# One graph-network block on one core: edge transfers in halves, finer waits in the reduction trees, one more chunk's sums on TensorE, first group merged tile by tile

## The chip, the cores and the metric

One core of a Trainium2 chip. The metric is the device time of one execution in microseconds, the median of several.

## The reference

Inputs are 6250 nodes with 256 features, 200,000 edges with 96 features, sorted by destination, and the weights of three layers. What is computed:

```
xn   = layernorm(x)                                   # (6250, 256)
sum, max, cnt = segment sum / max / count of edge_attr_96 by dst      # (6250, 96) each
h    = [xn, sum, max (0 where cnt = 0), sum / max(cnt,1), u]          # 256+3*96+64
gnn  = relu(h @ W1 + b1) @ W2 + b2 + xn
q,k,v = split(xn @ Wqkv + bqkv);  q, k centred by row, squared, normalised
mix  = (v + q2 @ (k2^T @ v) / sqrt(N)) @ Wout + bout                  # linear attention
x1   = x + gnn + mix
xm   = layernorm(x1);  w = xm @ wr + br
the 3124 nodes of largest w get  gelu(xm @ w1 + b1) @ w2 + b2, times w, on top
out  = x1 + xm + (that, for chosen nodes)
```

All of it in float32, or in products of split float32 parts (high and low) on TensorE.

## The kernel before, in words

**Edges.** The edges are padded to 448 x 448 = 200,704 = 128 x 1568 rows. Each partition holds 1568 consecutive edges, cut into 49 chunks of 32 edges. Four edges make a quad. `edge_chunk(c)` on VectorE works on one chunk of 128 x 32 x 96 in a buffer `xb` (four of them): a tree of two steps for the maximum (L995 into `mx`, L999) and two for the sum (L998, L1002, in place) reduces each quad to one row, and then a running segmented scan goes over the chunk's eight quads: for each quad a maximum (L1018) and a sum (L1021), each with a per-partition flag that restarts a segment, into `ob` (two buffers). The semaphore `s_tree` counts tree steps, `s_max` and `s_sum` count scan steps. Before its tree a chunk waits for its load (`s_load`), and before its scan for the dump of the chunk two back (`s_dump`), and for all four tree steps.

SyncE loads chunk c + 4 and dumps chunk c to `scan_d` in DRAM once chunk c is scanned (`dump_and_load`): one dump of 768 KB and one load of 1536 KB a chunk, in this order in its queue. Between chunks 36 and 41 SyncE adds loads of W1 (four pieces), W2 (two) and the tail rows.

**Sums on TensorE.** For the chunks in `SUMS` (1, 2, and 44 to 48) VectorE leaves the two sum steps out. `quad_sums(c)` on TensorE adds the four edges of each quad with identity matmuls, four quads (a half) into one PSUM bank. The sum scan then reads PSUM. Chunks 1 and 2 share the banks `psKx`, the late ones `psR` and `psC`, so each half waits until the chunk before has been scanned that far.

**Nodes, beside the edges.** ScalarE takes the root for the layer norm (L1555), behind two small DMA issues (L1551, L1553) that wait for VectorE. VectorE finishes the deviations, and goes on with chunk 1. TensorE and ScalarE then go over 12 groups of 4 tiles of 128 nodes and one tile more: transposes, queries and keys, the base rows, key products. VectorE gives key norms at fixed chunks (`NORM`), the last two behind chunks 32 and 33. GpSimd gathers neighbour rows of destinations, from which ScalarE and VectorE find each node's segment.

After chunk 35 VectorE gives the factors `s_fac`, and TensorE and ScalarE do the attention product of the 13 groups: fetch 512 KB of `qT_d` on ScalarE's queue (four buffers), product, scaled copy, store 512 KB to `att_d` on the same queue. Between groups `WORK` spreads the rounding of the weights to a high part (ScalarE, `h0` to `h5`) and low parts (TensorE product and ScalarE copy, `l0` to `l11`). `h4` and `h5` need both W2 loads. `quad_sums(44)` stands behind group 10. The sums of chunks 45 to 48 stand behind the last attention group, its evacuation and a product with `endrow`, with one piece of the W1 tail product (`tail_part(0)` to `(3)`) behind each; ScalarE copies these out (`tail_rows`).

**Ramp into the node stage.** GpSimd gathers the raw first and last quads of group 0's segments (`raw0`). ScalarE waits for the last attention store, copies tail parts 0 and 1, rounds the node columns, then masks raw rows: 24 products into `graw[1]` (L1773) and 24 into `kept` (L1779). Behind these it issues the loads of `xTr[1]`, `bg` and `tg` (L1783, L1786), and copies tail parts 2 and 3. VectorE, once chunk 48 is scanned, makes a scan over partitions for segments that cross them (L1085 to L1088, L1262), then `aggregate(0, 0, 0, 2)`, `carries()`, `aggregate` parts 3 and 4 over all four tiles at once, `repair()` of rows in `scan_d`, and `aggregates_low`. GpSimd gathers the scan rows of group 0 (`grow`) with one semaphore for the four when all dumps have landed, then the row for the repair, the raw rows of group 1, writes the repair, four small constants, and goes on with the gathers of later groups. TensorE does the node products of group 0 for four pieces, transposes all four tiles of merged rows, and goes on with `turn(0, 4)`.

**Node stage and last network.** Thirteen turns on TensorE: hidden layer in split products, output in split products; VectorE, ScalarE and GpSimd merge the next group's edge rows beside it. Then the selection of nodes, and the last network over the chosen ones.

## Time and profile before

| | |
|---|---|
| median of 3 runs | 1180.55 us (1180.41 to 1182.44) |
| the profiled execution | 1180.66 us |
| its span, first to last instruction | 1178.9 us |
| busy: TensorE, VectorE, ScalarE, GpSimd | 1051.5, 991.9, 500.4, 451.9 us |
| mean granted TensorE clock | 0.938 |
| moved by DMA | 234.99 MB, mean 199 GB/s |

The times of all rows are microseconds from the start of the span. The span is 1.8 us shorter than the execution. Busy shares are averages over stages: VectorE's comes from the edge chunks (to 492 us), TensorE's from the node stage behind them.

### The profile page before, as it was taken

How to read it: one execution, taken by the hardware profiler on the slowest of the kernel's cores; microseconds unless marked ns; L12 is line 12 of the kernel's file. 1: busy time of each engine (PE TensorE's matmuls, PEld its weight loads, DVE VectorE, ACT ScalarE, POOL GpSimd, SP SyncE). 2: the span in 40 equal slices, each digit the busy share in tenths (PEclk: the TensorE clock that was granted, in tenths of full speed). 3: DMA queues.
4: the chain of work that ended last, by engine and by line, in shares of the span. 5: the costliest groups of instructions: out<-in, count | busy, mean ns of one | idle time of the engine just before them, and what ended most of it. 6: DMA issues, size and time to landing. Idle time of an engine off the chain costs nothing.

```text
span 1178.9 us, 16127 instructions
## 1 busy us (share of the span) xinstructions
PE 1051.5 (89%) x4683; PEld 781.9 (66%) x4683; DVE 991.9 (84%) x2410; ACT 500.4 (42%) x1487; POOL 451.9 (38%) x344
## 2 busy tenths in 40 slices
PE   2598999999988759888999999999999986799996
PEld 1355555656635536466888888888888972488886
DVE  7899999999999997966988889888897757576574
ACT  3547877778832422611332233322333323243341
POOL 0088810888300002076565445654443000223331
PEclk9798999999996979979999999999999996599998
DMA  9799999999988999533443333433333130111110
GB/s 344 288 318 371 346 376 365 356 376 360 335 315 330 415 418 366 189 120 90 133 148 127 123 102 126 150 124 125 107 102 123 54 108 17 38 37 42 46 43 20
DMA packets 76512, 234.99 MB, mean 199 GB/s; under 512 B 13105, under 2 KB 43094, under 8 KB 70178
## 3 DMA queue, kind: packets, MB, share of 16 engines
q1 hardware_dynamic: 42786, 157.00, 35.7%
q0 software_dynamic: 14224, 33.61, 10.0%
q10 hardware_dynamic: 19440, 43.66, 9.9%
q8 instruction: 26, 0.43, 0.2%
q14 instruction: 36, 0.29, 0.1%
HBM read 153.68 MB, written 80.55 MB: 199 GB/s over the span
## 4 chain that ended last, share of the span: by engine, by line
PE 49%; DVE 3%; POOL 2%; issue 1%; DMA 0%; ACT 0%; DVEq 0%; POOLq 0%
PE psR L70 5%; PE psC L70 5%; PE psQ L59 5%; PE psQ L60 5%; PE psKx L59 5%; PE psQ L61 5%; PE psKx L60 5%; PE psKx L61 5%; PE psR L71 3%; PE psC L71 2%; PE psT L2168 1%; PE psQ L2189 1%; PE psKx L2189 1%; POOL graw L474 1%; PE psR L69 1%
## 5 line engine op out<-in xcount | busy, mean ns | idle before, releaser
L474 POOL DMA_INDIRECT graw<-in_edge_attr,ic x90 | 128.7, 1430 | 33.1 <-issue 24.1
L1018 DVE SCALAR_TENSOR_TENSOR ob<-ob,mQ,mx 128x96 f32<-128x96 f32 x392 | 122.3, 312 | 13.4 <-PE psR L1943 6.5
L684 POOL DMA_INDIRECT near<-in_dst,rowi x49 | 87.8, 1792 | 63.8 <-DVEq L924 49.1
L1818 ACT ACTIVATE hT_hi<-psQ 128x512 fp32r<-128x512 f32 (+2 forms) x52 | 29.9, 575 | 186.0 <-PE psQ L2189 142.5
L684 POOL DMA_INDIRECT near<-ends_d,blki x49 | 82.3, 1679 | 68.0 <-DVEq L915 53.4
L1021 DVE SCALAR_TENSOR_TENSOR ob<-ob,kQ,xb 128x96 f32<-128x96 f32 x336 | 104.5, 311 | 0.0
L1970 PE MATMUL psQ<-Wqk,xT 128*128 128x512 f32 (+1 forms) x196 | 94.3, 604 | 0.0
L995 DVE TENSOR_TENSOR mx<-xb 128x1536 f32<-128x1536 f32 x49 | 85.6, 1747 | 1.2 <-DVE carry L1076 0.2
L998 DVE TENSOR_TENSOR xb<-xb 128x1536 f32<-128x1536 f32 x42 | 73.8, 1758 | 1.4
L500 POOL DMA_INDIRECT grow<-scan_d,ic x49 | 54.0, 1101 | 42.8 <-DMA scan_d<-ob 28.1
L70 PE MATMUL psR<-W2w,hT_hi 128*128 128x512 f32 x175 | 65.7, 411 | 3.9 <-DVE x L1184 3.9
L1818 ACT ACTIVATE hT_hi<-psKx 128x512 fp32r<-128x512 f32 (+2 forms) x52 | 29.8, 575 | 88.8 <-PE psKx L2189 88.7
L788 POOL DMA_INDIRECT out_x<-zo,lst x25 | 24.6, 986 | 104.7 <-DVE zo L1474 104.7
L70 PE MATMUL psC<-W2w,hT_hi 128*128 128x512 f32 x168 | 60.8, 399 | 0.0
L1991 PE MATMUL psKx<-xn,kc 128*128 128x257 f32 (+1 forms) x196 | 52.3, 390 | 5.2 <-ACT kc L1594 5.2
L480 POOL DMA_INDIRECT yg<-yrow_d,lst x25 | 24.9, 997 | 82.0 <-DVE lst L1426 74.7
L746 POOL COPY ic<-idx 128x12 int32 (+3 forms) x11 | 4.5, 407 | 134.5 <-PE psC L69 134.5
L1970 PEld LDWEIGHTS psQ<-Wqk,xT 128*128 128x128 f32 (+1 forms) x196 | 38.0, 194 | 26.9 <-issue 24.3
L1982 PE MATMUL psC<-WvoI,xT 128*128 128x256 f32 (+1 forms) x196 | 50.6, 381 | 0.0
L71 PE MATMUL psR<-W2w,hT_lo 128*128 128x256 f32 x175 | 49.9, 285 | 0.0
L71 PE MATMUL psC<-W2w,hT_lo 128*128 128x256 f32 x168 | 47.4, 282 | 0.0
L1174 DVE SCALAR_TENSOR_TENSOR hT_lo<-psQ,hT_hi 128x512 fp32r<-128x512 f32 (+2 forms) x52 | 34.0, 654 | 15.3 <-ACT hT_hi L1818 15.3
(533 smaller groups left out, 3284.4 us busy)
## 6 DMA issues: line engine op xcount, KB each, us to landing
xb<-in_edge_attr SPq DMA_DIRECT2D x49, 1536.0 KB
scan_d<-ob SPq DMA_DIRECT2D x49, 768.0 KB
yrow_d<-yr SPq DMA_DIRECT2D x48, 132.0 KB
xg<-in_x ACTq DMA_DIRECT2D x12, 512.0 KB
xT_d<-xT ACTq DMA_DIRECT2D x12, 512.0 KB
base_d<-dcur ACTq DMA_DIRECT2D x12, 512.0 KB
qT_d<-qT ACTq DMA_DIRECT2D x12, 512.0 KB
out_x<-xres SPq DMA_DIRECT2D x48, 128.0 KB
```

The costliest lines, as they stand in the source:

```text
L59: nc.tensor.matmul(out, lh, rh, start=start, stop=False)
L60: nc.tensor.matmul(out, lh, rl, start=False, stop=False)
L61: return nc.tensor.matmul(out, ll, rh, start=False, stop=stop)
L70: nc.tensor.matmul(out, lh, both.rearrange("p h n -> p (h n)"), start=start, stop=False)
L71: return nc.tensor.matmul(out[:, 0:NF], ll, both[:, 0, :], start=False, stop=False)
L474: nc.gpsimd.indirect_dma_start(out=to.rearrange("p i f -> p (i f)"), out_offset=None, in_=raw_v, in_offset=bass.IndirectOffsetOnAxis(ap=ic ...
L684: nc.gpsimd.indirect_dma_start(out=near[:, t, :], out_offset=None, in_=table, in_offset=bass.IndirectOffsetOnAxis(ap=rows[:, t:t + 1], axi ...
L995: nc.vector.tensor_tensor(mx[:, :, :, :], xp[:, :, :, 0, :], xp[:, :, :, 1, :], ALU.max).then_inc(s_tree, 1)
L998: nc.vector.tensor_tensor(xp[:, :, :, 0, :], xp[:, :, :, 0, :], xp[:, :, :, 1, :], ALU.add).then_inc(s_tree, 1)
L1018: nc.vector.scalar_tensor_tensor(o[:, q, 0:EF], prev[:, 0:EF], mQ[:, bass.ds(c * TQ + q, 1)], mx[:, q, 0, :], ALU.min, ALU.max).then_inc(s ...
L1021: nc.vector.scalar_tensor_tensor(o[:, q, EF:AGG], prev[:, EF:AGG], kQ[:, bass.ds(c * TQ + q, 1)], quad_sum, ALU.mult, ALU.add).then_inc(s_ ...
L1970: ins = nc.tensor.matmul(o, xT[:, c, t * P:t * P + rows], Wqk[:, c, :], start=False, stop=(c == KF - 1))
```

## The change

- **Transfers in halves.** Loads and dumps of a chunk become two each, of 16 edges or 4 quads a partition. For each half of the scan done, SyncE issues half a dump and half a load. All semaphore counts double.
- **Trees.** The first sum step no longer waits for the first maximum step; each later step waits for the one two back; the scan's first maximum waits for the maximum tree, its first sum for the sum tree.
- **Roots sooner.** ScalarE's root stands ahead of the two small DMA issues.
- **Chunk 2's sums.** First half into `psR`, issued behind chunk 1's sums without a wait for its scan; second half into `psKx[0]`, issued inside TensorE's first node turn.
- **Chunk 42's sums** go to TensorE, behind attention group 9; those of 44 behind group 10, of 45 ahead of the last group. Tail part 0 now stands behind 46, part 1 behind 47, parts 2 and 3 behind 48.
- **Weights.** W1 in two pairs behind chunks 36 and 37, W2 behind 38 and 39, tail rows behind 40. `h4` and `h5` two groups later, `l8` to `l11` one later. The rows to gather are found behind chunk 38 instead of 39.
- **Ramp.** GpSimd makes the constants before the scan gathers; each tile's scan gather has its own semaphore. VectorE merges what doesn't need scan rows first, then tile by tile (`first_rows`): the zero for a node without edges comes through `unkept`, the mean from the mean of the other parts. TensorE transposes two tiles, does the fourth piece of node products, then the other two tiles. The loads of `xTr[1]`, `bg`, `tg` move from ScalarE's queue to SyncE's.

The core of the diff:

```diff
-SUMS_LATE = (44, 45, 46, 47, 48)
+SUMS_LATE = (42, 44, 45, 46, 47, 48)
...
-            psS = {c: psKx if c in SUMS_EARLY else [psR, psC] for c in SUMS}
+            psS = {c: [psR, psC] for c in SUMS_LATE}
+            psS[SUMS_EARLY[0]], psS[SUMS_EARLY[1]] = psKx, [psR, psKx[0]]
...
-            WORK = {4: ("h0",), 5: ("h1", "l0", "l1"), 6: ("h2", "l2", "l3"), 7: ("h3", "l4", "l5"), 8: ("h4", "l6", "l7"),
-                    9: ("h5", "l8", "l9"), 10: ("l10", "l11")}
+            WORK = {4: ("h0",), 5: ("h1", "l0", "l1"), 6: ("h2", "l2", "l3"), 7: ("h3", "l4", "l5"), 8: ("l6", "l7"),
+                    10: ("h4", "l8", "l9"), 11: ("h5", "l10", "l11")}
...
                 def dump_and_load(c, b, load):
-                    sp.wait_ge(s_sum, c * TQ + TQ + 1)
-                    sp.wait_ge(s_max, c * TQ + TQ + 1)
-                    sp.dma_start(scan_v[:, quads(c), :], ob[b % OB][:, :, :]).then_inc(s_dump[b % OB], 16)
-                    if load:
-                        sp.dma_start(xb[b][:, :, :, :].rearrange("p q i f -> p (q i) f"),
-                                     ev[:, bass.ds(c * T + XB * T, T), :]).then_inc(s_load[b], 16)
+                    for h in range(2):
+                        sp.wait_ge(s_sum, c * TQ + 4 * h + 5)
+                        sp.wait_ge(s_max, c * TQ + 4 * h + 5)
+                        sp.dma_start(scan_v[:, bass.ds(c * TQ + 4 * h, 4), :], ob[b % OB][:, 4 * h:4 * h + 4, :]).then_inc(s_dump[b % OB], 16)
+                        if load:
+                            sp.dma_start(xb[b][:, 4 * h:4 * h + 4, :, :].rearrange("p q i f -> p (q i) f"),
+                                         ev[:, bass.ds(c * T + XB * T + 16 * h, 16), :]).then_inc(s_load[b], 16)
...
-                pool.wait_ge(s_dump[0], 16 * 25)
-                pool.wait_ge(s_dump[1], 16 * 24)
-                gather_scan(0, GT, P, s_g0s)
+                pool.wait_ge(s_dump[0], 16 * 50)
+                pool.wait_ge(s_dump[1], 16 * 48)
+                for t in range(GT):
+                    nc.gpsimd.indirect_dma_start(
+                        out=grow[0][:, t, :], out_offset=None, in_=scan_d,
+                        in_offset=bass.IndirectOffsetOnAxis(ap=ic[0][:, 2, t:t + 1], axis=0)).then_inc(s_g0[t], 16)
...
                     nc.vector.tensor_tensor(mx[:, :, :, :], xp[:, :, :, 0, :], xp[:, :, :, 1, :], ALU.max).then_inc(s_tree, 1)
+                    if not on_pe:
+                        dve.wait_ge(s_tree, n0)
+                        nc.vector.tensor_tensor(xp[:, :, :, 0, :], xp[:, :, :, 0, :], xp[:, :, :, 1, :], ALU.add).then_inc(s_tree, 1)
                     dve.wait_ge(s_tree, n0 + 1)
-                    if not on_pe:
-                        nc.vector.tensor_tensor(xp[:, :, :, 0, :], xp[:, :, :, 0, :], xp[:, :, :, 1, :], ALU.add).then_inc(s_tree, 1)
                     nc.vector.tensor_tensor(mx[:, :, 0, :], mx[:, :, 0, :], mx[:, :, 1, :], ALU.max).then_inc(s_tree, 1)
...
-                    dve.wait_ge(s_tree, n0 + (2 if on_pe else 4))
+                    dve.wait_ge(s_tree, n0 + (2 if on_pe else 3))
...
+                        if q == 0 and not on_pe:
+                            dve.wait_ge(s_tree, n0 + 4)
...
+                    def first_rows():
+                        each = rcnt[:, 0:GT].rearrange("p (t o) -> p t o", o=1).broadcast_to([P, GT, EF])
+                        step(nc.vector.tensor_tensor(graw[0][:, :, 1, :], graw[0][:, :, 1, :], graw[0][:, :, 2, :], ALU.add), False)
+                        step(nc.vector.tensor_tensor(kept[:, :, 0, :], kept[:, :, 0, :], kept[:, :, 1, :], ALU.max))
+                        step(nc.vector.tensor_tensor(graw[0][:, :, 2, :], graw[0][:, :, 1, :], each, ALU.mult))
+                        for t in range(GT):
+                            dve.wait_ge(s_g0[t], 48)
+                            sums, mean_ = grow[0][:, t, EF:AGG], graw[0][:, t, 2, :]
+                            nc.vector.tensor_tensor(agg[:, t, EF:2 * EF], kept[:, t, 0, :], grow[0][:, t, 0:EF], ALU.max).then_inc(s_lead, 1)
+                            nc.vector.tensor_tensor(agg[:, t, 0:EF], graw[0][:, t, 1, :], sums, ALU.add).then_inc(s_lead, 1)
+                            nc.vector.scalar_tensor_tensor(agg[:, t, 2 * EF:3 * EF], sums, rcnt[:, t:t + 1], mean_, ALU.mult, ALU.add).then_inc(s_lead, 1)
...
                     aggregate(0, 0, 0, 2)
+                    dve.wait_ge(s_am, 2)
+                    dve.wait_ge(s_as, 2)
+                    step(nc.vector.tensor_tensor(kept[:, :, 1, :], kept[:, :, 1, :], kept[:, :, 2, :], ALU.max), False)
+                    step(nc.vector.tensor_tensor(graw[0][:, :, 2, :], graw[0][:, :, 2, :], graw[0][:, :, 3, :], ALU.add))
                     carries()
-                    for part in range(3, 5):
-                        aggregate(0, 0, 0, part)
+                    first_rows()
+                    for t in range(2):
+                        aggregates_low(0, t)
                     repair()
+                    for t in range(2, GT):
+                        aggregates_low(0, t)
...
+                act.wait_ge(s_ln, 1)
+                nc.scalar.sqrt(sd[:, :], va[:, :]).then_inc(s_sqrt, 1)
                 act.wait_ge(s_bw, 2)
...
+                QUADS_BEHIND = {9: 42, 10: 44}
...
+                quad_sums(45)
                 attention(GROUPS, 0, GROUPS // 4 * 16 + 16)
...
-                for i in range(4):
-                    quad_sums(SUMS_LATE[1 + i])
+                for i in range(3):
+                    quad_sums(46 + i)
                     tail_part(i)
+                tail_part(3)
...
-                    for m in range(4):
+                    for m in range(3):
                         hidden_nodes(0, m)
-                    transposes(0, range(GT))
+                    transposes(0, range(2))
+                    hidden_nodes(0, 3)
+                    transposes(0, range(2, GT))
```

## Rows read from the trace of the kernel before

**Rows 1.** Two stretches: us, TensorE, weight loads, VectorE, ScalarE, GpSimd busy (x), PEclk, DMA share, GB/s

```profile
200.00:250.00 50.00, 50.00 (x205) 31.50 (x204) 49.05 (x117) 36.85 (x130) 39.85 (x23) 1.00 0.97 360
420.00:440.00 20.00, 6.82 (x27) 4.58 (x25) 19.22 (x60) 3.91 (x8) 0.00 (x0) 0.80 1.03 415
```

**Rows 2.** Who waited for whom: us in total, times, longest

```profile
DVE ob L1018 <- PE psR L1943: 6.5, 1, 6.5
DVE a L901 <- ACT sd L1555: 2.2, 1, 2.2
DVE ob L1018 <- PE psC L1943: 1.4, 4, 0.5
DVE ob L1018 <- PE psKx L1943: 1.3, 2, 0.8
...
ACT W2w L1717 <- DMA rW<-in_L_gnn_W: 15.0, 1, 15.0
```

**Rows 3.** VectorE's timeline, chunk 34: start, us, line, operation, idle before

```profile
349.36 1.74 DVE L995 TENSOR_TENSOR mx<-xb 128x1536 f32<-128x1536 f32 x1
351.14 1.76 DVE L998 TENSOR_TENSOR xb<-xb 128x1536 f32<-128x1536 f32 x1
352.81 0.95 DVE L999 TENSOR_TENSOR mx<-mx 128x768 f32<-128x768 f32 x1
353.68 0.95 DVE L1002 TENSOR_TENSOR xb<-xb 128x768 f32<-128x768 f32 x1
354.72 0.32 DVE L1018 SCALAR_TENSOR_TENSOR ob<-ob,mQ,mx 128x96 f32<-128x96 f32 x1
...
358.40 1.75 DVE L995 TENSOR_TENSOR mx<-xb 128x1536 f32<-128x1536 f32 x1
```

**Rows 4.** VectorE's timeline: end of chunk 35, chunks 47 and 48, merging

```profile
367.45 0.16 DVE L1055 TENSOR_SCALAR kcol<-kcol 128x2 f32<-128x2 f32 x1
...
479.07 1.76 DVE L995 TENSOR_TENSOR mx<-xb 128x1536 f32<-128x1536 f32 x1
...
485.55 1.75 DVE L995 TENSOR_TENSOR mx<-xb 128x1536 f32<-128x1536 f32 x1
...
496.12 1.36 DVE L1120 TENSOR_TENSOR kept<-kept 128x1152 f32<-128x1152 f32 x1 [0.35 <-DVE carry L1262]
...
505.77 0.56 DVE L1128 TENSOR_TENSOR kept<-kept,grow 128x384 f32<-128x384 f32 x1 [4.78 <-issue]
```

**Rows 5.** ScalarE's timeline: the root's table load, the masking

```profile
45.75 1.28 ACT L1555 ACT_TABLE_LOAD   x1 [2.03 <-DVEq L867]
...
479.61 6.48 ACT L1773 ACTIVATE graw<-raw,kSel 128x96 f32<-128x96 f32 x24
485.99 8.69 ACT L1779 ACTIVATE kept<-raw,unkept,kSel 128x96 f32<-128x96 f32 x24
```

**Rows 6.** TensorE's timeline: first node group, tail product, group 0's edge products, turn 0

```profile
62.37 0.60 PE L1956 MATMUL psT<-ident,xn 128*128 128x128 f32 x4
...
476.26 1.02 PE L2103 MATMUL psQ<-rW1t,ident 96*98 96x512 f32 x2
...
477.99 2.42 PE L1943 MATMUL psR<-xb,ident 128*128 128x384 f32 x7
...
515.33 0.77 PE L59 MATMUL psQ<-aggT_hi,W1f_hi 128*128 128x512 f32 x1 [1.49 <-DVE tailT L1160]
...
548.36 0.80 PE L70 MATMUL psR<-W2w,hT_hi 128*128 128x512 f32 x1 [3.92 <-DVE x L1184]
```

**Rows 7.** SyncE's timeline: the first W load and the fifth

```profile
379.97 1.99 SPq L596 DMA_DIRECT2D rW<-in_L_gnn_W  x2
...
407.65 0.44 SPq L599 DMA_DIRECT2D rW<-in_L_gnn_W  x1
```

**Rows 8.** DMA issues in 376 to 380 and 405 to 412: KB each, us to landing

```profile
rW<-in_L_gnn_W SPq DMA_DIRECT2D x1, 512.0 KB, 11.7
rW<-in_L_gnn_W SPq DMA_DIRECT2D x1, 512.0 KB, 22.7
```

More of the change, by code:

```diff
@@ L488, in wait_chosen @@
                 if g == 0:
-                    engine.wait_ge(s_g0[t], 32 + 16)
+                    engine.wait_ge(s_g0[t], 48 + 16)
                 elif t == 0:
@@ L604, in _ @@
                         sp.dma_start(ub[GF:GF + 1, :], b1.rearrange("(a b) -> a b", a=1)).then_inc(s_wl[5], 16)
+                sp.wait_ge(s_at, 6 + KF + 12 * GT)
+                for e in range(4):
+                    sp.wait_ge(s_t2o[e], 16 * (GROUPS // 4 + (e == 0)))
+                for t in range(GT):
+                    sp.wait_ge(s_g0[t], 48)
+                sp.dma_start(xTr[1][:, :, :], xT_d[1:2, :, :, :].rearrange("o p c n -> p (o c) n")).then_inc(s_ld[1], 16)
+                for e in range(2):
+                    for to, src in ((bg[e], base_d), (tg[e], att_d)):
+                        sp.dma_start(to[:, :, :].rearrange("p t f -> p (t f)"), src[e * P:(e + 1) * P, :]).then_inc(s_lb[e], 16)
                 def node_stage():
@@ L1067, in _ @@
                         ends_of_segments()
-                    if c == 39:
+                    if c == 38:
                         rows_to_gather()
@@ L1076, in _ @@
                         step(nc.vector.memset(carry[:, 2 * EF:2 * EF + 1], 1.0))
+                        step(nc.vector.tensor_tensor(unkept[:, :, 5], unkept[:, :, 5], has[:, 0:GT], ALU.mult))
                         dve.sem_inc(s_lead, 1)
@@ L1274, in node_stage @@
                     dve.wait_ge(s_u, 1)
-                    for t in range(GT):
-                        aggregates_low(0, t)
                     selection_constants()
@@ L1933, in _, with quad_half @@
                 ins.then_inc(s_wv, 1)
+                def quad_half(c, h):
+                    pe.wait_ge(s_load[c % XB], c // XB * 32 + 32)
+                    group = SUMS_EARLY if c in SUMS_EARLY else SUMS_LATE
+                    k = group.index(c)
+                    if c == SUMS_EARLY[1]:
+                        pe.wait_ge(s_bw, 2)
+                        if h == 1:
+                            pe.wait_ge(s_sum, SUMS_EARLY[0] * TQ + 5)
+                    elif k:
+                        pe.wait_ge(s_sum, group[k - 1] * TQ + 4 * h + 5)
+                    for i in range(4):
+                        ins = nc.tensor.matmul(psS[c][h][:, 0:4 * EF], ident[:, :], xb[c % XB][:, 4 * h:4 * h + 4, i, :],
+                                               start=(i == 0), stop=(i == 3))
+                    ins.then_inc(s_wv if c in SUMS_EARLY else s_pt, 1)
                 def quad_sums(c):
-                    pe.wait_ge(s_load[c % XB], c // XB * 16 + 16)
                     for h in range(2):
-                        if c not in (SUMS_EARLY[0], SUMS_LATE[0]):
-                            pe.wait_ge(s_sum, (c - 1) * TQ + 4 * h + 5)
-                        for i in range(4):
-                            ins = nc.tensor.matmul(psS[c][h][:, 0:4 * EF], ident[:, :], xb[c % XB][:, 4 * h:4 * h + 4, i, :],
-                                                   start=(i == 0), stop=(i == 3))
-                        ins.then_inc(s_wv if c in SUMS_EARLY else s_pt, 1)
+                        quad_half(c, h)
                 def transpose_nodes(g, t):
@@ L2017, in turn @@
                         base(g, t)
+                        if g == 0 and t == 0:
+                            quad_half(SUMS_EARLY[1], 1)
                         if t + 2 < nt:
@@ L2029, in _ @@
                 pe.wait_ge(s_wrb, 3)
-                for c in SUMS_EARLY:
-                    quad_sums(c)
+                quad_sums(SUMS_EARLY[0])
+                quad_half(SUMS_EARLY[1], 0)
                 pe.wait_ge(s_wq, 1)
@@ L2136, in _ @@
                 nc.tensor.matmul(psT[0][:, :], ones[:, :], endrow[:, :], start=True, stop=True).then_inc(s_t, 1)
-                for i in range(4):
-                    quad_sums(SUMS_LATE[1 + i])
+                for i in range(3):
+                    quad_sums(46 + i)
                     tail_part(i)
+                tail_part(3)
                 pe.wait_ge(s_max, CHUNKS * TQ + 1)
@@ L2159, in transposes @@
                         for t in tiles:
-                            if t == 0:
+                            if isinstance(g, int) and g == 0:
+                                pe.wait_ge(s_lead, 2 + 5 * (t + 1))
+                            elif t == 0:
                                 pe.wait_ge(s_am, g * NAM + NAM)
```

72 lines of the change are left out of this document (38 added, 34 removed).

## The prediction

> **What bounds the kernel now.** I read the page's slices first, then the busy time by stretches, the waits, and last the timelines of the engines around the places that the change touches. From 50 to 492 us VectorE is the bound: in a typical stretch it is busy 49.05 of 50 us, and it folds one edge chunk after another [rows 1]. Afterwards TensorE is (100 us busy in 100 from 600 to 900). So the time is the end of the edge chunks, plus a ramp in which TensorE waits for the first group's merged rows, plus two stages that the change leaves alone. The ramp's end, H, is TensorE's first edge product of group 0, at 515.33 [rows 6]. What the change is worth is how far H moves, plus what it does to one stall behind H.
>
> VectorE's own waits inside the edge stage are few: 2.2 us for ScalarE's root, 1.3 for the sums of chunk 2, 6.5 and 1.4 for late chunks' sums [rows 2]. It never waits for a load or a dump, though the DMA engines are busy 0.97 to 1.03 of the time and move 360 to 415 GB/s [rows 1]. That is cover which can be used up, and the change uses some of it.
>
> **Start.** ScalarE's table load for the root begins at 45.75, behind two DMA issues that wait for VectorE, and VectorE waits 2.2 us for it [rows 2, 5]. The root now goes ahead of both, so about 2.0 of that go. Chunk 2's first half of sums gets a bank of its own and no longer waits for chunk 1, and TensorE reaches its second half at about 54 instead of VectorE needing it at 59: the 1.3 us go. TensorE's first node group starts near 50 instead of 62.37 [rows 6]; with the half inserted in it its lead is about 8.6 us. That gains nothing by itself. It lets TensorE keep up with a VectorE that is 12 us earlier where the key norms (chunks 32, 33) release it.
>
> **Trees.** In a chunk folded by VectorE the four tree instructions start at 349.36, 351.14, 352.81, 353.68 and the scan at 354.72 [rows 3]. The steps behind a wait for the instruction just ahead are 1.78 and 1.04; those without such a wait are 1.67 and 0.87. Reordered, each wait has another instruction in between: 1.78 becomes 1.67 and 1.04 becomes 0.87, 0.28 us a chunk. Bounds: 0, if the sum scan then exposes the same latency (it comes 1.10 behind the last sum, and 1.04 was enough), and 0.28. I take 0.28, on the 41 chunks that stay on VectorE: 11.5 us.
>
> **Chunk 42 on TensorE.** 9.04 us a chunk [rows 3] becomes 6.48, as chunk 47 takes from 479.07 to 485.55 [rows 4]: 2.6 us. TensorE pays about 5.3 (a half is eight passes, seven take 2.42 [rows 6]), in a stretch where it idles.
>
> **Late sums.** The 6.5 us wait came from chunk 45's sums queued behind the last attention group and its evacuation, and that behind a 15.0 us wait of ScalarE for the W2 rows [rows 2]. Now W2 is requested a chunk earlier and rounded two groups later, and 45's sums go ahead of that group. 6.5 us go. The 1.4 of small waits for psC I leave in: TensorE's 5.3 plus 1.7 of tail product (476.26 to 477.99 [rows 6]) still make some 7 us a chunk against 6.48. Moving the gather rows from chunk 39 to 38 changes no sum; one small multiply adds 0.1.
>
> So without DMA effects the last chunk would end 2.0 + 1.3 + 11.5 + 2.6 + 6.5 - 0.1 = 23.8 us earlier.
>
> **What the DMA gives back.** SyncE's queue lags in the attention stage. The first W row, issued at 379.97, lands 11.7 later; the one at 407.65 takes 22.7 [rows 7, 8]. Between these landings (391.7 and 430.4) that queue moved 0.52 MB of W1 and three times 2.88 MB (dump, load, W), 9.2 MB in 38.7 us: 237 GB/s. A chunk of 9.04 us asks for 318. Before, the prefetch of three chunks covered it. Now chunks ask every 8.76 us, and the full wait for the dump two chunks back bites first, since its second half stands behind half a load. My ledger: chunk 35 ends at 367.45 [rows 4] less 12.8 = 354.6; the factors and small work keep their lengths; chunk 40 ends at 404.2 and chunk 41's scan wants dump 39 at 409.3. The queue delivers the second W1 pair at 394.2, W2's first half at 406.4, and dump 39 (1.57 MB on) at 413.0: 3.7 us late. Dump 40 is 0.4 late, later ones are not, as ScalarE's queue then runs dry. The raw rows' gathers now fall into the same stretch; I give them 1. Sum 5.0, bounds 0 (the queue gets more than 237) and 10 (it gets 200). Chunk 48 ends 18.8 us earlier, about 473.5. Issuing in halves by itself costs SyncE some 1.7 us in 8.8 and waits for nobody.
>
> **The ramp.** Here I expect a loss that pays for the merging. ScalarE's masking (6.48 and 8.69 us) starts at 479.61 before, just behind the second tail product [rows 5, 6]. That product now stands behind chunk 47's sums instead of 46's, and those can't finish before chunk 46 is scanned: half a sum 1.8 us before its end, then 5.3, 0.4 of lag, 1.7 of product, 1.6 of ScalarE's copies, so masking starts 7.2 us after chunk 46, not 1.3 (that chunk ended 0.8 ahead of 479.07 [rows 4]). It ends 8.5 us behind the last chunk (492.3: chunk 48 from 485.55, 6.48 and small waits [rows 4]) instead of 2.4, and VectorE's merging, which began 3.8 behind it at 496.12, starts 4.8 later [rows 4]. From there H came 19.2 us later, 4.8 of which VectorE waited for the scan rows (at 505.77 [rows 4]). That wait is gone: half dumps and gathers behind single tiles have landed long before. The pieces added (two steps ahead of the carries, three in front of the tiles, twenty small ones) take 5.7 us against 4.2 of whole-group ones, but the first two tiles' transposes and casts run beside the last ones. I cost that as even: H is 14.4 behind the start of merging. H moves by 18.8 - 4.8 + 4.8 = 18.8 us. Bounds of the ramp's own part: 4.8 better (ScalarE in time), 3 worse. ScalarE loses 2.2 us of DMA issues; that helps TensorE's node products start, not H. SyncE's loads of group 0 and 1 now come after masking and gathers, wanted 30 us later.
>
> **Behind H.** TensorE waits at 548.36, 3.92 us for VectorE and that for GpSimd's addition, which is the end of an unbroken row of gathers [rows 6]. GpSimd now starts its scan gathers sooner and is 1.3 us earlier against H. Its iotas moved into an idle stretch. So 1.3 us go: 1180.66 (the profiled execution, 0.1 over the median of the runs) less 18.8 + 1.3 = 20.1 gives 1160.5. The node stage and the last network I leave as they are.
>
> **A page's rule.** While SyncE's queue moves its 237, all queues move about 415 [rows 1]: some 178 go to the others, ScalarE's rows of 4 KB a partition above all, against SyncE's of 12 and 6 KB. The Trainium skill (DMA: Bandwidth & Descriptors, Queues, rings and completion order) says that each DMA engine takes turns between queues packet by packet. By that rule halved edge packets cost SyncE's queue part of its share; the second rival below is this mechanism.
>
> **Rivals.**
> *No DMA lateness, or ScalarE not late in the ramp.* For it: no wait for a dump or load stands in the profile. Against: the 22.7 us landing. It gives back 5 to 6: 1155. Chance 0.17.
> *Halved packets lose turns.* Loads and dumps are then nearer in size to the other queue's rows, and the 237 fall to some 205. Dump 39 is 8 us late instead of 3.7: 1165. For it: a third to a half of the rate goes to a queue that has far smaller rows. Against: no row shows who is served in which order, and 237 may be what SyncE's transfers get whatever their size. Chance 0.15.
> *The edge stage is already DMA-bound.* The share of 0.97 to 1.03 then means no spare rate, and faster trees only wait. 34 chunks times 0.28 = 9.5 are lost: 1170. Against it: 415 GB/s in one stretch, 360 in the other [rows 1]. Chance 0.10.
> *Slower: halves lower the DMA rate.* A chunk needs 2.36 MB, and the node groups some 0.8 MB, in 8.76 us: 361 GB/s from chunk 3 on. Above that nothing is lost; at 338 the 299 us of chunks 3 to 35 grow by 20 and the gain is gone; at 330 the time is 1189. That is a fifth under the 415 shown. Chance 0.05, with small other mishaps. The same skill page (Rules for kernel authors) advises 1 MiB or more per DMA for full bandwidth, which speaks against halves; no row here shows a cost of 768 KB transfers.
> *Nothing measurable,* because gains are given back in an unread place: 1180, 0.03.
> My forecast: 0.50, own range 1156 to 1165.
>
> **How the numbers follow.** 1160.5 is the likeliest. With the first rival 1153 is the low end, with the packet and bound cases 1170 the high one; under 0.2 lie outside. A difference under 0.2% (2.4 us) can't be told from none. Faster 0.92, same 0.03, slower 0.05.
>
> **What would show it.** Tree steps of 1.67 and 0.87 throughout; the root's wait and chunk 2's gone; chunk 35 ending near 354.6. Waits of VectorE for a dump around chunk 41, 3 to 5 us. Masking starting some 7 us behind chunk 46, and VectorE's first merge waiting for ScalarE. H near 496.5; the stall of 3.92 us near 2.6. I am wrong if chunks of 8.76 us don't appear from chunk 3 on, if the last chunk ends after 480, or if the stretch behind H takes other than 662 to 664 us.

## Result: 4% slower, and the profile after

| | before | after |
|---|---|---|
| time, median | 1181.21 us (4 runs) | 1228.35 us (1224.36 to 1231.53, 4 runs) |
| profiled execution, span | 1180.66, 1178.9 us | 1231.53, 1229.6 us |
| H, TensorE's first edge product of group 0 | 515.33 [rows 6] | 567.80 |

The ratio is 1.0396, 95% interval 1.0358 to 1.0435: slower, where I had forecast 1160.5 us, faster. All of it lies ahead of H. The stretch behind H fell from 663.6 to 661.8 us. One stray execution each of two kernels below, 3618.39 and 2101.27 us, counts in the median of its kernel and not in its ratio; without it these medians are 1176.59 instead of 1177.58 and 1171.51 instead of 1172.41 us.

The waits of the changed kernel (engine and line waiting <- what ended the wait: us in total, times, longest) show where VectorE stands now. Of these lines, the first three had no counterpart before; the wait for psR was 6.5 us and the one for ScalarE's root (tile sd) 2.2 us [rows 2].

```profile
DVE rk L1048 <- ACT junk L1655: 61.1, 5, 29.2
...
DVE ob L1036 <- DMA scan_d<-ob: 10.3, 2, 5.6
...
DVE kept L1141 <- ACT kept L1824: 4.6, 1, 4.6
...
DVE ob L1036 <- PE psR L1989: 2.2, 2, 1.4
DVE cT L1106 <- PE psC L2199: 2.2, 1, 2.2
...
DVE a L918 <- ACT sd L1597: 0.3, 1, 0.3
```

VectorE waits 61.1 us for ScalarE's sums of squares, which make the keys' norms: no such wait stood in the profile before. ScalarE's own waits lead one step further back, to GpSimd's gathers:

```profile
ACT jc L1561 <- DMA near<-ends_d,blki: 33.1, 4, 17.2
ACT jc L1570 <- DMA near<-in_dst,rowi: 28.4, 2, 21.7
```

The gathered rows (tile near) show why they are late. First the kernel before: count, duration of an issue min/median/max in ns, first and last start.

```profile
L684 POOL DMA_INDIRECT near<-ends_d,blki x49: 943/1484/3890, 57.4 to 153.3; - x49
L684 POOL DMA_INDIRECT near<-in_dst,rowi x49: 1015/1486/3891, 203.4 to 302.0; - x49
```

The same two groups in the changed kernel:

```profile
L694 POOL DMA_INDIRECT near<-ends_d,blki x49: 940/1365/8447, 56.3 to 194.4; - x49
...
L694 POOL DMA_INDIRECT near<-in_dst,rowi x49: 940/1361/8442, 228.9 to 352.4; - x49
```

Same count, a lower median, but a longest issue of 8.4 us instead of 3.9: 138.1 and 123.5 us from first to last start instead of 95.9 and 98.6. VectorE and GpSimd side by side, in the changed kernel:

```profile
102.02 1.44 POOL L694 DMA_INDIRECT near<-ends_d,blki  x1 [0.30 <-issue]
103.76 8.44 POOL L694 DMA_INDIRECT near<-ends_d,blki  x1 [0.30 <-issue]
112.50 8.43 POOL L694 DMA_INDIRECT near<-ends_d,blki  x1 [0.30 <-issue]
```
```profile
106.22 1.75 DVE L1012 TENSOR_TENSOR mx<-xb 128x1536 f32<-128x1536 f32 x1
107.89 1.75 DVE L1015 TENSOR_TENSOR xb<-xb 128x1536 f32<-128x1536 f32 x1
109.56 0.95 DVE L1017 TENSOR_TENSOR mx<-mx 128x768 f32<-128x768 f32 x1
110.43 0.95 DVE L1020 TENSOR_TENSOR xb<-xb 128x768 f32<-128x768 f32 x1
111.30 0.31 DVE L1036 SCALAR_TENSOR_TENSOR ob<-ob,mQ,mx 128x96 f32<-128x96 f32 x1
```

The trees do what I predicted: steps of 1.67, 1.67, 0.87 and 0.87, 8.74 us from tree to tree (106.22 to 114.96). But an issue that begins 2.46 us ahead of a tree (103.76) now ends at 112.20, in the scan behind it; the next begins at 112.50, at the same place in the pattern, and is as long. Before, the longest one began 1.33 us ahead of a tree and ended 0.78 us into the second step:

```profile
90.48 3.89 POOL L684 DMA_INDIRECT near<-ends_d,blki  x1 [0.30 <-issue]
```
```profile
91.81 1.75 DVE L995 TENSOR_TENSOR mx<-xb 128x1536 f32<-128x1536 f32 x1
93.59 1.76 DVE L998 TENSOR_TENSOR xb<-xb 128x1536 f32<-128x1536 f32 x1
95.27 0.95 DVE L999 TENSOR_TENSOR mx<-mx 128x768 f32<-128x768 f32 x1
```

Between 91.81 and 93.59 lie 1.78 us instead of 1.67: the gap of 0.11 that the change took away. And where VectorE sits idle for the norms, each issue takes 0.94 us (the nine that begin from 124.91 to 134.89 all do). A stretch of the changed kernel with such a wait, columns as in [rows 1]: VectorE is busy 8.02 of 20 us.

```profile
120.00:140.00 20.00, 2.94 (x14) 1.71 (x13) 8.02 (x22) 6.18 (x24) 16.34 (x13) 0.65 0.68 208
```

The ramp, in VectorE's, ScalarE's and TensorE's timelines, as in [rows 4 to 6]:

```profile
552.55 1.36 DVE L1141 TENSOR_TENSOR kept<-kept 128x1152 f32<-128x1152 f32 x1 [4.62 <-ACT kept L1824]
```
```profile
537.25 6.47 ACT L1818 ACTIVATE graw<-raw,kSel 128x96 f32<-128x96 f32 x24
543.63 8.68 ACT L1824 ACTIVATE kept<-raw,unkept,kSel 128x96 f32<-128x96 f32 x24
```
```profile
567.80 0.47 PE L59 MATMUL psQ<-aggT_hi,W1f_hi 128*128 128x512 f32 x1 [1.49 <-DVE tailT L1181]
...
599.14 0.79 PE L70 MATMUL psR<-W2w,hT_hi 128*128 128x512 f32 x1 [5.17 <-DVE x L1205]
```

### The profile page after: what moved, and what is told of

It reads as the page before. It is cut to its first block, busy times and chain, and to the rows that moved or that the text cites. A ratio compares the mean times of both kernels' runs of the same rounds, so it can differ in the third digit from the quotient of the medians.

```text
span 1229.6 us, 16562 instructions
## 1 busy us (share of the span) xinstructions
PE 1062.3 (86%) x4699; PEld 787.4 (64%) x4699; DVE 984.4 (80%) x2424; ACT 502.0 (41%) x1487; POOL 533.9 (43%) x344
## 4 chain that ended last, share of the span: by engine, by line
PE 47%; DVE 3%; POOL 1%; issue 1%; DMA 0%; ACT 0%; DVEq 0%; POOLq 0%
PE psR L70 5%; PE psC L70 5%; PE psQ L59 4%; PE psQ L60 4%; PE psQ L61 4%; PE psKx L59 4%; PE psKx L60 4%; PE psKx L61 4%; PE psR L71 3%; PE psC L71 2%; PE psT L2225 1%; PE psQ L2246 1%; PE psKx L2246 1%; POOL graw L472 1%; PE psR L69 1%
## 5 line engine op out<-in xcount | busy, mean ns | idle before, releaser
L694 POOL DMA_INDIRECT near<-ends_d,blki x49 | 124.4, 2539 | 66.9 <-DVEq L932 52.3
L694 POOL DMA_INDIRECT near<-in_dst,rowi x49 | 117.3, 2394 | 48.1 <-DVEq L941 33.5
L1036 DVE SCALAR_TENSOR_TENSOR ob<-ob,mQ,mx 128x96 f32<-128x96 f32 x392 | 122.3, 312 | 14.1 <-DMA scan_d<-ob 10.3
L2020 PE MATMUL psQ<-Wqk,xT 128*128 128x512 f32 (+1 forms) x196 | 95.9, 613 | 0.0
L70 PE MATMUL psR<-W2w,hT_hi 128*128 128x512 f32 x175 | 66.2, 414 | 5.2 <-DVE x L1205 5.2
L2056 PE MATMUL psT<-ident,q 128*128 128x128 f32 (+1 forms) x98 | 19.0, 307 | 49.9 <-ACT qT L1696 49.7
L70 PE MATMUL psC<-W2w,hT_hi 128*128 128x512 f32 x168 | 60.8, 399 | 0.0
L498 POOL DMA_INDIRECT grow<-scan_d,ic x45 | 52.2, 1160 | 15.2 <-issue 13.4
L2041 PE MATMUL psKx<-xn,kc 128*128 128x257 f32 (+1 forms) x196 | 55.6, 409 | 0.0
L2032 PE MATMUL psC<-WvoI,xT 128*128 128x256 f32 (+1 forms) x196 | 53.1, 395 | 0.0
L1048 DVE TENSOR_SCALAR rk<-k2s 128x4 f32<-128x4 f32 (+1 forms) x13 | 2.4, 186 | 61.1 <-ACT junk L1655 61.1
L2056 PEld LDWEIGHTS psT<-ident,q 128*128 128x128 f32 (+1 forms) x98 | 11.0, 150 | 62.2 <-issue 60.1
```

The lines of the kernel that those rows point to most:

```text
L70: nc.tensor.matmul(out, lh, both.rearrange("p h n -> p (h n)"), start=start, stop=False)
L694: nc.gpsimd.indirect_dma_start(out=near[:, t, :], out_offset=None, in_=table, in_offset=bass.IndirectOffsetOnAxis(ap=rows[:, t:t + 1], axi ...
L1036: nc.vector.scalar_tensor_tensor(o[:, q, 0:EF], prev[:, 0:EF], mQ[:, bass.ds(c * TQ + q, 1)], mx[:, q, 0, :], ALU.min, ALU.max).then_inc(s ...
L2020: ins = nc.tensor.matmul(o, xT[:, c, t * P:t * P + rows], Wqk[:, c, :], start=False, stop=(c == KF - 1))
```

## Experiments

Theory A: GpSimd's gather issues get through only where VectorE leaves a gap behind an instruction that the next one waits for; the finer waits took those gaps out of the tree. Rival B: the halved transfers slow the gathers. All times are medians, ratios are to the kernel before on the same chip. The kernels ran on four chips, on which the kernel before took 1179.2 to 1181.4 us; where two runs come from different chips, the ratios are the fairer comparison.

### Trees or transfers

Only the tree waits undone (chunk 42, halves, root, merging kept):

```
-    wait(n0);     sum1;  wait(n0+1); max2;  wait(n0+2); sum2;  wait(n0+3); scan...
+    wait(n0+1);   sum1;              max2;  wait(n0+2); sum2;  wait(n0+4); scan...
```


> The changed kernel with one part undone: the tree's four instructions in the old order with the old waits (two of them behind the instruction just ahead); halves, chunk 42 on TensorE, the root and the merging stay. Theory A (GpSimd's gathers pass only in the gaps that VectorE leaves behind such waits): near gathers' issues are back at a mean of 1.7 to 1.8 us and a maximum of 3.9, the 49 gathers of each array take 96 to 99 us instead of 138 and 124, VectorE's wait for the key norms (61.1 us) is gone, and the time is 1165 to 1178. Rival B (the halved transfers slow the gathers): the issues stay at 2.4 to 2.5 us, the wait stays above 45 us, and the time is 1215 or more, since the trees only get 11 us slower and the wait hides that.

1177.58 us, ratio 0.9959 (0.9945 to 0.9973). Issues are back at a median of 1484 ns, 3892 the longest, and there is no wait for the norms. That is A's case and not B's; the time is at the upper edge of what I expected.

The kernel before with the finer tree waits alone:

```
-    wait(n0+1); sum1;             max2; ... wait(n0+4); scan
+    wait(n0);   sum1; wait(n0+1); max2; ... wait(n0+3); scan max 0; wait(n0+4); scan sum 0
```


> The kernel before with one part alone: the tree's reordered instructions and finer waits. Theory A: near gathers' issues go to a mean of 2.4 us and a maximum of 8.4, a wait of VectorE for the key norms of 40 to 65 us appears, and the time is 1215 to 1235, slower than before. Rival B: issues stay at 1.7 to 1.8 us with a maximum of 3.9, no such wait, and the trees' 0.28 us in 41 chunks make it 1168 to 1172.

1247.47 us, ratio 1.0507 (1.0437 to 1.0576), above A's range. This one edit alone costs more than the whole change does. Its near issues and its wait:

```profile
L684 POOL DMA_INDIRECT near<-ends_d,blki x49: 941/1367/8444, 57.4 to 196.9; - x49
L684 POOL DMA_INDIRECT near<-in_dst,rowi x49: 941/948/8449, 226.2 to 338.7; - x49
```
```profile
DVE rk L1031 <- ACT junk L1613: 74.7, 5, 46.9
```

The changed kernel with whole transfers for loads and dumps (`for h in range(2)` of SyncE's loads and dumps undone, semaphore counts halved):

> The changed kernel with one part undone: edge chunks loaded and scan rows dumped in whole transfers again. Theory A: near gathers still take 2.4 to 2.5 us each with a maximum of 8.4, the key-norm wait stays above 50 us, and the time is 1218 to 1234. Rival B: issues are back at 1.7 to 1.8 us, the wait is gone, and the time is 1160 to 1170.

1244.44 us, ratio 1.0514 (1.0447 to 1.058): B falls; issues still reach 8.4 us and the wait for the norms is 86.3 us (in an execution of 1255.87 us). The time is above A's range too: without the halves it is even slower than the changed kernel, and I have no reason for that.

Both undone:

> Both undone: old tree waits and whole transfers, with chunk 42 on TensorE, the root, the late sums and the merging tile by tile kept. Against the run with old trees alone it gives the worth of the halves. By my ledger (dump waits of 10.3 us in the changed kernel, caused by SyncE's queue being behind): if the halves cause the lateness, the dump waits shrink below 3 us and this kernel is 3 to 8 us faster than the one with old trees and halves; if the lateness is only one of bytes per time, both have the same waits within 2 us, and this one is 0 to 3 us slower, for the later loads and dumps in the ramp. If rival B holds for the gathers, this kernel is the only one of the four near 1165.

1176.0 us, ratio 0.9953 (0.9935 to 0.9971). Waits for dumps 2.3 instead of 5.8 us, waits for late sums (psR) 2.9 instead of 1.3, the same time as with halves within the intervals. The dump waits fell as in my first case and the time stayed as in my second, so neither case came out whole. The halves are worth nothing measurable here.

### Which gap

The changed kernel, `wait(n0+1)` ahead of the first sum put back, nothing else:

> The changed kernel, with the tree's first wait alone put back: the first sum waits for the first maximum just ahead of it (0.11 us of gap a tree); the others stay a step apart. In the kernel before, issues that begin late in a scan (7.7 us behind the tree's start) end 2.55 to 2.6 us behind the next tree's start, 0.9 behind that gap. If this gap is what lets them through, near issues have a maximum of 3.9 and a mean of 1.8 again, the key-norm wait is gone, and the time is 1168 to 1174: that with old trees less 0.17 us in each of 41 trees, part of it given back in waits for dumps. If one gap a tree isn't enough, the mean is above 2.2 and the time above 1195.

1169.56 us, ratio 0.9918 (0.9886 to 0.9949). No wait for the norms, as expected, but the longest issue is 5.0 us, not 3.9:

```profile
L694 POOL DMA_INDIRECT near<-ends_d,blki x49: 949/1487/5034, 55.5 to 164.4; - x49
L694 POOL DMA_INDIRECT near<-in_dst,rowi x49: 1064/1487/5030, 197.5 to 305.4; - x49
```

The changed kernel, `wait(n0+4)` ahead of the scan put back instead:

> The changed kernel, with the tree's last wait alone put back: the scan waits for the last sum just ahead of it (0.17 us of gap a tree); the first sum goes on behind the first maximum without a gap. If it is the gap behind the first maximum that ends the long issues, this one does not help: near issues still reach 8.4 us, and the time is 1215 to 1235. If any gap in the tree will do, the mean falls to 1.9 or less with a maximum near 7, and the time is 1170 to 1180.

1199.26 us, ratio 1.0157 (1.0125 to 1.0189), between my two cases. The longest issue is 7.3 us, as in my second case, and 25.8 us of waits for the norms stay:

```profile
DVE rk L1046 <- ACT junk L1653: 17.4, 3, 10.9
...
DVE rk L1046 <- ACT k L1650: 8.4, 2, 6.2
```

So 0.11 us a tree, behind the first maximum, do more than 0.17 us ahead of the scan: it is the place of the gap that counts. VectorE's and GpSimd's timelines of the four kernels (before, changed, these two) tell what each gap does. I take the issues that are under way when a tree starts and are not through within 0.81 us:

| gap behind the first maximum | gap ahead of the scan | such issues | the longest begin ahead of the tree, us | end behind its start, us | longest, us |
|---|---|---|---|---|---|
| yes | yes (before) | 12 | 1.31 to 1.33 | 2.56 to 2.58 | 3.89 |
| yes | no | 14 | 2.45 to 2.47 | 2.56 to 2.58 | 5.03 |
| no | yes | 14 | 1.31 to 1.32 | 5.97 to 5.98 | 7.30 |
| no | no (changed) | 14 | 2.45 to 2.47 | 5.97 to 5.99 | 8.45 |

The first gap decides the end: with it such an issue ends 0.9 us behind the first tree instruction, without it only behind all four (5.08 us). The second gap decides the beginning: with it the last issue ahead of the tree begins 1.3 us before it, without it the longest ones begin 2.46 us before it and don't get through in the rest of the scan either. One issue of each kind with one gap only:

```profile
157.26 5.03 POOL L694 DMA_INDIRECT near<-ends_d,blki  x1 [0.30 <-issue]
```
```profile
105.35 7.29 POOL L694 DMA_INDIRECT near<-ends_d,blki  x1 [0.30 <-issue]
```

The "only" in theory A is too strong, though. An issue that begins inside a tree mostly gets through without any gap: of 31 such issues of the changed kernel 30 take 2.44 us at most. Here one begins in the first step (97.50) and ends at 100.06, 0.91 us behind the start of the second, and the next ends at 101.72, 0.90 behind the start of the third; no gap lies between these steps.

```profile
98.42 1.64 POOL L694 DMA_INDIRECT near<-ends_d,blki  x1 [0.30 <-issue]
100.36 1.36 POOL L694 DMA_INDIRECT near<-ends_d,blki  x1 [0.30 <-issue]
```
```profile
99.15 1.75 DVE L1015 TENSOR_TENSOR xb<-xb 128x1536 f32<-128x1536 f32 x1
100.82 0.95 DVE L1017 TENSOR_TENSOR mx<-mx 128x768 f32<-128x768 f32 x1
```

The finer waits only where GpSimd gathers no near rows:

```
+    calm = 13 <= c <= 17 or c >= 30      # finer waits here, the old ones elsewhere
```


> The changed kernel, with the finer waits kept only in chunks 13 to 17 and from 30 on, where GpSimd has no near rows to gather; the others wait as in the kernel before, with the sum behind the first maximum. Theory A: no key-norm wait, near issues mean 1.7 to 1.8 us; 18 trees are 0.28 us shorter (5.0 us) and VectorE's waits for dumps give back 2 to 4 of it, so 1 to 3 us under the kernel with old trees. If the finer waits cost something outside the gathers too, it is not faster than that one.

1171.26 us, ratio 0.9922 (0.9894 to 0.9949), 6.3 us under the old trees (4.4 by the ratios), more than expected. The profiled executions differ by 5.8. VectorE's last chunk ends 2.5 us sooner (trees 5.0, less 1.0 of dump waits, 0.8 of psR and 0.7 that I can't place). The rest is behind the merging: TensorE's wait for GpSimd, 2.13 us with old trees, is 0.35 (below), and its work from H to that wait is 1.3 us shorter. The last gather of the first kind of near rows ran into a tree without gaps and took 7.3 us; no other took more than 3.9.

### The ramp

TensorE's second tail product ahead of chunk 47's sums, old trees:

> The kernel with the old tree waits, and TensorE's second tail product ahead of chunk 47's sums instead of behind them. If the ramp's loss is the order of the tail products, as I predicted, ScalarE's masking (480.89 to 495.97 with old trees alone) starts 5 to 6.5 us sooner, VectorE's first merge starts at about 491.6 instead of 496.20, right behind its own carry work, and the time is 4 to 5 us under the one with old trees (1171 to 1173 in a profiled run). Rival: the merging then waits for the gathers of the last scan rows instead (they end near 498 on GpSimd), and the gain is under 1.5 us.

1177.36 us, ratio 0.9961 (0.9941 to 0.9981): nothing. Masking began 2.5 us sooner only. In the profiled execution, the slowest of eleven (1181.22 us), VectorE ended its last chunk 4.6 us later: it waited 1.9 us more for dumps and 1.3 more for sums (those of chunks 47 and 48 now stand behind one more product), and 0.9 us were lost ahead of chunk 38. ScalarE's masking ahead of its four tail copies, tail products 2 and 3 behind the carries, on the kernel with the first gap:

> The kernel with the first gap put back, and ScalarE's masking ahead of all four of its tail copies, so that it waits for no tail product; TensorE makes the last two tail products behind the carries instead of between the sums. In the kernel with the first gap the masking runs from 475.26 to 490.3 and VectorE's first merge starts at 490.57, while its carry work ended at 486.0 and had waited 2.2 us for TensorE. Theory (the ramp's loss is masking behind the tail products): masking starts at about 468 to 469, as soon as chunk 46 is scanned, the first merge starts at 484 to 486, H comes 4 to 6 us sooner, and the time is 1163 to 1166. Rival: the merging then waits for the gathered scan rows (issued from 486.6 to 491.3) and H moves by less than 2 us.

1177.35 us (1171.33 to 1180.18), ratio 0.9952 (0.9925 to 0.9978). The first merge started at 484.18 instead of 490.57, as expected, but H came at 508.73 instead of 507.94, as my rival had it and for another reason. ScalarE's first cast of a transposed tile came only at 502.80, 4.7 us behind the end of the first two tiles' transposes (the six at 497.56, behind which the next product starts at 498.13).

SyncE's five loads for groups 0 and 1 held until the last cast, alone and with that:

```
+    sp.wait_ge(s_al, 2 * GT)   # ahead of the loads of xTr[1], bg, tg
```


> The kernel with the first gap put back, and SyncE's five loads of 0.5 MB for groups 0 and 1 held until the last aggregate of group 0 is cast (they are issued in the ramp otherwise, and the DMA share is 1.00 to 1.02 from 494 to 504). In that kernel ScalarE's casts of the third and fourth tile begin 1.9 us and more behind their transposes, in the changed kernel 0.6. If the burst of loads delays them, first merge to H falls from 17.4 us to about 15.2, and the time by 2 us, to 1167 to 1168. If it is something else, H stays and the stall behind it may grow (the loads come later): 1169 to 1172.

1175.2 us, ratio 0.9936 (0.991 to 0.9961). The DMA share beside the casts fell from 1.0 to 0.5, and the third cast came 4.3 us behind the second as it had without the hold (2.9 in the changed kernel): the loads are not it. A wait for the norms of 10.1 us is back, with the same tree as the run of 1169.56.

> Both of these: masking first and loads held, with the first gap put back. If the two gains add, 1161 to 1164. If the gathered scan rows end last in the ramp, it is the same as the better of the two within 1 us.

1176.91 us (1169.51 to 1180.8), ratio 0.996 (0.9936 to 0.9983): they don't add, and 3.4 us of waits for norms are there.

> Masking first, loads held, and the first gap put back only where GpSimd gathers near rows (chunks 0 to 12 and 18 to 29), the trees of chunks 13 to 17 and from 30 on wait as in the changed kernel. 18 trees are 0.11 us shorter, 2.0 us, of which the waits for dumps give back about half: 1160 to 1163, 1 us under the kernel with both. Near issues stay at a mean of 1.9 to 2.0. If the finer waits late in the edge stage cost GpSimd's raw gathers more than they bring, it is not faster.

1185.42 us (1175.92 to 1195.28), ratio 1.0032 (1.0004 to 1.0061), far above the 1160 to 1163 that I had expected. Here the one gap stood only where near rows are gathered, and the gathers, slower than with two gaps, ran on beyond chunk 12 into trees with none: the longest issue was 8.4 us again.

```profile
L695 POOL DMA_INDIRECT near<-ends_d,blki x49: 946/1488/8443, 55.7 to 169.7; - x49
```

One gap a tree is thus no safe repair: how it meets the issues changes with what else is moved, and from run to run (1169 to 1177 us for one kernel). With the two gaps during the gathers the ramp can be read cleanly. Masking first on that tree:

> The kernel with the finer waits only where GpSimd has no near rows to gather, with ScalarE's masking ahead of its tail copies (as with the single gap before). Trees are steady here, so the ramp alone is read. If only the order of ScalarE's work mattered, first merge starts 6 us sooner and H 4 to 6 us sooner, 1165 to 1167. If, as the single-gap pair showed, the casts of the transposed tiles come late instead, the first merge starts 6 us sooner but H stays within 2 us: 1169 to 1174.

1172.54 us, ratio 0.9949 (0.9932 to 0.9966). H came at 504.95 instead of 510.79, 5.8 us sooner, the casts 0.52 us behind their transposes, and still no gain: TensorE then waits at its next product.

```profile
504.95 0.54 PE L59 MATMUL psQ<-aggT_hi,W1f_hi 128*128 128x512 f32 x1 [1.54 <-DVE tailT L1184]
...
539.76 0.79 PE L70 MATMUL psR<-W2w,hT_hi 128*128 128x512 f32 x1 [6.42 <-DVE x L1208]
```

The calm-tree kernel without it:

```profile
510.79 0.76 PE L59 MATMUL psQ<-aggT_hi,W1f_hi 128*128 128x512 f32 x1 [3.43 <-DVE tailT L1184]
...
538.35 0.50 PE L70 MATMUL psR<-W2w,hT_hi 128*128 128x512 f32 x1 [0.35 <-DVE x L1208]
```
GpSimd's addition that VectorE waits for (L773) begins at 534.70 without the sooner masking and at 536.45 with it.

In the kernel before, the changed one, that with old trees and the five on calm trees, 629 to 631 us follow TensorE's product at L70. GpSimd's row from the scatter of the repaired rows to that addition, broken only by the wait for the scatter to land, takes 27 to 31 us in them, and TensorE waits at L70 for it in each, 0.35 to 6.42 us. In this pair a sooner H only lengthened that wait. The same with GpSimd's raw gathers of group 1 held until the casts:

> The same as the one with calm trees and masking first, and GpSimd's eight raw gathers of group 1 held until the last tile of group 0 is cast, so that nothing is gathered beside the casts but SyncE's loads. If those gathers delay the casts, the casts come 0.6 us behind their transposes, and first merge to H falls from 18 to 25 us to 15 to 16; the time is then set by group 1's rows, needed some 5 us behind H and now there 12 behind it: the stall behind H grows by 4 to 8 us. If they don't, the casts stay 2 to 5 us late and the time is 1175 or more.

1184.17 us, ratio 1.0029 (1.0014 to 1.0044), in the range of my second case but without its late casts: the addition came 12.0 us later, and so did L70 (551.80). The casts were on time in both, so it does not tell what delays them elsewhere.

### The dumps

Weight rows asked for a chunk later, as before, on the calm trees:

> The kernel with the finer waits only where GpSimd has no near rows to gather, and SyncE's loads of the weight rows (W1, W2, tail rows) put back a chunk later, where they were before. There VectorE waits 4.70 us at 412.19 and 2.05 us at 423.27 for dumps. My ledger (bytes on SyncE's queue): the dumps wait behind those rows, so these two waits fall to 0 to 3 us together and the last chunk ends 3 to 5 us sooner, time 1167 to 1169. Rival: the rows then come too late, ScalarE's roundings and TensorE's sums of the late chunks are queued behind them, and waits for sums (psR) take the place of the dumps': 1170 to 1174.

1170.85 us, ratio 0.9928 (0.9912 to 0.9945). The two waits fall from 4.70 and 2.05 to 3.30 and 1.10 us, but three more appear (0.60, 2.01, 2.22): 9.2 us in all, and the waits for sums are gone. The time is in my rival's range, but its reason (waits for sums in place of those for dumps) is refuted. The bytes move the wait, they don't remove it.

> The kernel with the finer waits only where GpSimd has no near rows to gather, and whole transfers for chunks and dumps. With old trees whole transfers had dump waits of 2.3 instead of 5.8 us and the same time. If halves cost the queue its rate, the waits for dumps are 3 us or more under the 6.8 of the halves and the time is 1 to 3 us lower (1168 to 1170); if bytes per time set them, 1170 to 1174.

1172.41 us, ratio 0.9935 (0.9915 to 0.9954): dumps 4.5 instead of 6.8, sums (psR) 5.0 instead of 2.1. As with the old trees, the wait changes its place and the time stays.

## Why the prediction was wrong

The step that failed is "Trees". It is right for VectorE (0.28 us a chunk) and wrong by omission: I bounded it by 0 and 0.28 us, gave no reason why it could not be a loss, and let every other engine keep its pace, though GpSimd was busy 39.85 of 50 us beside it [rows 1]. I never asked what GpSimd did in VectorE's gaps. Removing 0.28 us a chunk, 11.5 us in all, cost 61.1 us of waits.

The rest of the sum was too hopeful by less. Without the trees' 11.5 us it gives 1172.0 us, and that kernel, with old trees, took 1177.58. There the last chunk ended 5.8 us sooner than before, not 7.3, and H came only 1.8 us sooner (513.52), since first merge to H took 17.3 us and not 14.4: ScalarE's casts came late. Behind H it then was 3.4 us shorter, not 1.3.

From the forecast H (496.5) to the measured one (567.80) are 71.3 us:

| term | forecast | measured | off by |
|---|---|---|---|
| waits for key norms | 0 | 61.1 | 61.1 |
| waits for dumps | 5.0 (0 to 10) | 10.3 | 5.3 |
| late sums, other small terms up to the last chunk's end (473.5 / 542.8) | 1.4 | 3.2 in waits for sums, the rest not placed | 2.9 |
| last chunk's end to end of masking | 8.5 | 9.5 | 1.0 |
| first merge to H | 14.4 | 15.25 | 0.9 |

(542.8 - 473.5 = 69.3 is the sum of the first three; 0.1 is rounding.)

Point by point. **Start**: held. The root's wait is 0.3 instead of 2.2, chunk 2's is gone; with the old trees chunk 35 begins at 355.08 instead of 358.40 [rows 3], 3.3 sooner, just 2.0 + 1.3. **Chunk 42**: held, 6.5 us from its tree to the next (491.08 to 497.61). **Late sums**: the 6.5 us wait is gone; 2.2 us for psR and 1.0 for psC are left, not 1.4. **Dumps**: the waits came, with a size at the upper bound and one chunk earlier than in my ledger (chunks 40 and 41: 5.65 and 4.69 us). The ledger itself isn't borne out: with the weight rows a chunk later, where it gave 0 to 3 us, they were 9.2 us in all. Neither the halves nor the time of the weight rows is the cause by itself: whole transfers took 3.5 and 2.3 us off these waits and added 1.6 and 2.9 to those for psR. **Ramp**: right in kind. Masking ended 9.5 us behind the last chunk and the merge waited 4.62 us for it. But it paid nothing to know: moved out of the way, it gained 5.8 us at H and none at the end. **Behind H**: wrong. GpSimd's addition did come 1.7 us sooner against H (28.0 instead of 29.7 us behind it), but TensorE was done with what it had 2.9 us sooner against H (26.2 instead of 29.1 us), so its stall grew from 3.92 [rows 6] to 5.17 us. TensorE's granted clock (PEclk, behind GpSimd's busy time) in the stretch from H was 0.95 of full speed instead of 0.91, first the changed kernel, then the one before:

```profile
567.80:600.00 32.20, 26.79 (x127) 21.85 (x128) 24.04 (x54) 7.89 (x17) 25.72 (x19) 0.95 0.27 77
```
```profile
515.33:548.00 32.67, 28.47 (x124) 23.00 (x124) 23.18 (x50) 7.67 (x17) 26.78 (x25) 0.91 0.30 86
```

So "H plus 662 to 664" was missed by 0.2 us (661.80) and is no rule: it is 657.1 us in the calm-tree kernel (510.79 of 1167.9) and 673.2 where the raw gathers were held (509.50 of 1182.7). What counts is the later of H's products and GpSimd's row.

**The rivals.** None had this mechanism. The slower one (halves lower the DMA rate, 0.05) happened to have the sign, but whole transfers were no faster in any of three pairs. These pairs speak against *halved packets lose turns* as well, though no run shows the order in which the queues are served. *The edge stage is already DMA-bound* falls too: where no other wait stands, trees follow each other in 8.74 us.

By the Trainium skill (SBUF — State Buffer, Who interferes with whom) a VectorE instruction with two SBUF inputs contends with a GpSimd instruction that reads SBUF. By the Trainium skill (SBUF — State Buffer, Summary: rules for kernel authors) the one of the two that issues second is blocked until the first has finished. The trace agrees in part: issues take 0.94 us with VectorE idle and mostly 1.36 to 2.44 when they begin inside a tree. But 8.44 us is longer than any VectorE instruction beside it (1.75), so what counts there is not the end of one but whether another follows without a gap. The first of these sections also infers that such a VectorE instruction (`tensor_tensor`) does not hold up descriptor generation. Here the issues of gathers were held up beside it, and the measurement decides. That a port is the cause is argued, not shown: no run shows what an issue reads or writes, only how its length hangs on the gaps.

What stays open: why an issue that begins inside the tree passes at the next step without a gap, while one under way when the tree starts does not, and why without the second gap it is not through in the 2.46 us of scan ahead of the tree; what delays ScalarE's casts of the transposed tiles by 1.4 to 4.8 us in some kernels; and what would take SyncE's queue out of chunks 40 and 41.

The best versions are the first gap alone (1169.56 us, 0.9918) and the calm trees (1171.26 us, 0.9922; with the rows a chunk later 1170.85 us, 0.9928): three of one size within their intervals, all faster than both kernels, by under 1% against the one before. I would keep the calm trees, since the kernels with the first gap alone were unsteady: medians of 1169.56, 1175.2, 1176.91 and 1177.35 us.

## What to carry to other kernels

Before you close gaps on a saturated engine, look at who works in them: read the neighbour's instruction durations by where they fall in the pattern, not by their mean. Here the median fell while the maximum doubled. When a gain at the critical point doesn't arrive at the end, look for the second chain that was nearly as late; here 27 to 31 us of one engine's issues.

## What was not expected of the hardware

GpSimd's indirect DMA issues take 0.94 us beside an idle VectorE, 0.94 to 2.44 in most cases beside its edge work, and up to 8.45 us when VectorE's four tree instructions (5.08 us) follow each other without a dependent wait. With a gap of 0.11 us behind the first of them in every tree the longest is 5.03 us, with one of 0.17 behind the last 7.30, with both 3.89: the first gap sets where a held issue ends, the second how far ahead of the tree it begins. The issues fall into step with VectorE's pattern (two in a row of 8.44 and 8.43 us, both begun 2.46 us ahead of a tree).
